# Block-diagonal v in a macaron block: four masked ScalarE copies per chunk become one copy and four SBUF transfers

## The reference

```python
x = x + 0.5 * ffn(layernorm(x))           # 128 -> 512 -> relu -> 128
x = x + attn(layernorm(x))
x = x + 0.5 * ffn(layernorm(x))

q, k, v = split(x @ w_qkv.T)              # 8 heads x 16; blocks c of 32 tokens
qp = elu(q @ proj) + 1;  kp = elu(k @ proj) + 1      # 128 features f
kv   = einsum('bhcsf,bhcsd->bhcfd', kp, v)
num  = einsum('bhcsf,bhcfd->bhcsd', qp, kv)
z    = 1 / (einsum('bhcsf,bhcf->bhcs', qp, kp.sum(3)) + 1e-8)
out  = (num * z) @ w_out.T + b_out
```

## Time and profile before

| | us |
|---|---|
| median of 3 runs (132.30 to 133.36) | 132.82 |
| the profiled execution, its own time | 132.64 |
| its span, first to last instruction | 130.9 |
| PE busy (share) | 120.0 (92%) |
| ScalarE (ACT) busy | 90.3 (69%) |
| VectorE (DVE) busy | 89.6 (68%) |
| GpSimd (POOL) busy | 48.9 (37%) |
| granted TensorE clock | 1.000 |

### The profile page before, as it was taken

The page is one execution under the profiler, slowest core; times in us unless marked ns, Lnnn a source line. Parts: engine busy times, 40 slices in busy tenths (PEclk is TensorE's granted clock), DMA queues, the critical chain, the costliest instruction groups (busy, mean ns, idle before and its releaser), DMA issues.

```text
span 130.9 us, 4453 instructions
## 1 busy us (share of the span) xinstructions
PE 120.0 (92%) x1895; PEld 97.5 (75%) x1895; DVE 89.6 (68%) x223; ACT 90.3 (69%) x154; POOL 48.9 (37%) x54
## 2 busy tenths in 40 slices
PE   5989999959999988999998999999979979999891
PEld 5989989835759845876985685798557768788891
DVE  6899883495697579579569949961993694637411
ACT  4656395788897886878778887888787863351720
POOL 7635669069058049006205910930000048005300
PEclk9999999999999999999999999999999999999999
DMA  3898400993019200002900000570020000200202
GB/s 95 266 250 225 71 3 26 381 178 61 0 56 359 78 0 0 5 5 103 377 6 5 3 5 0 211 270 5 5 80 5 0 8 5 80 0 0 80 6 80
DMA packets 10123, 11.10 MB, mean 85 GB/s; under 512 B 788, under 2 KB 6296, under 8 KB 10104
## 3 DMA queue, kind: packets, MB, share of 16 engines
q1 hardware_dynamic: 9952, 10.75, 26.5%
q10 hardware_dynamic: 152, 0.07, 0.2%
HBM read 2.03 MB, written 1.05 MB: 24 GB/s over the span
## 4 chain that ended last, share of the span: by engine, by line
PE 76%; DVE 10%; ACT 6%; issue 6%; POOL 0%; POOLq 0%; DVEq 0%
PE G L310 17%; PE wide L336 9%; PE SO L347 6%; PE SO L363 5%; ACT expo L642 5%; PE G L319 4%; PE wide L389 4%; PE G L301 3%; PE G L292 3%; PE G L303 3%; PE G L302 3%; PE SO L310 3%; PE G L382 2%; DVE xnT_lo L815 2%; PE wide L301 2%
## 5 line engine op out<-in xcount | busy, mean ns | idle before, releaser
L828 DVE SCALAR_TENSOR_TENSOR feat<-expo,wide 128x1024 f32<-128x1024 f32 x32 | 38.7, 1218 | 19.6 <-ACT expo L642 19.3
L642 ACT ACTIVATE expo<-wide,minus_one 128x1024 f32<-128x1024 f32 x32 | 35.5, 1115 | 8.7 <-PE wide L336 8.6
L987 POOL TENSOR_TENSOR rstd<-var_eps,minus_half 128x4 f32<-128x4 f32 (+1 forms) x15 | 13.5, 899 | 65.5 <-DVE var_eps L801 65.2
L310 PE MATMUL G<-w,hidden 128*128 128x128 f32 x208 | 26.6, 277 | 0.0
L310 PEld LDWEIGHTS G<-w,hidden 128*128 128x128 f32 x208 | 25.1, 192 | 0.7
L336 PE MATMUL wide<-qk_packed,proj_padded 128*128 128x512 f32 x64 | 23.0, 444 | 0.4 <-DVE feat L828 0.3
L623 ACT ACTIVATE hidden<-G,b_cols 128x512 f32<-128x512 f32 (+1 forms) x25 | 16.0, 650 | 4.5 <-PE G L303 3.9
L347 PE MATMUL SO<-feat 128*32 128x32 f32 x1024 | 15.3, 197 | 1.4 <-DVE feat L828 1.3
L347 PEld LDWEIGHTS SO<-feat 128*32 128x32 f32 x1024 | 13.3, 111 | 2.3 <-DVE feat L828 1.7
L363 PEld LDWEIGHTS SO<-v_blocks,scores_sb 128*32 128x32 f32 x256 | 5.2, 108 | 12.3 <-issue 8.4
L363 PE MATMUL SO<-v_blocks,scores_sb 128*32 128x68 f32 x256 | 10.4, 234 | 2.8 <-DVE attn L844 1.8
(11 more groups left out here) (99 smaller groups left out, 193.5 us busy)
## 6 DMA issues: line engine op xcount, KB each, us to landing
qk_packed<-qk_hi SPq DMA_DIRECT2D x16, 256.0 KB, 2.5
qk_packed<-qk_lo SPq DMA_DIRECT2D x8, 256.0 KB, 2.5
qk_packed<-sixteenth SPq DMA_DIRECT2D x2, 512.0 KB, 6.3
x_in<-in_L_attn_x_dram SPq DMA_DIRECT2D x3, 256.0 KB, 5.2
out_dram<-x SPq DMA_DIRECT2D x3, 256.0 KB, 2.2
w<-in_L_ffn_W_dram SPq DMA_DIRECT2D x2, 256.0 KB, 4.1
x_in<-in_L_attn_x_dram SPq DMA_DIRECT2D x2, 128.0 KB, 2.6
proj_padded<-proj_hi SPq DMA_DIRECT2D x4, 64.0 KB, 2.5
```

The lines of the kernel that those rows point to most:

```text
L310: mm = pe.matmul(bank[:, t * D:(t + 1) * D], hidden[f][:, i, t * P:(t + 1) * P], w2[:, i, :], start=(i == 0 and t == tiles[0]), stop=(i == ...
L642: nc.scalar.activation(expo[:, n % 2, :, tokens(c)], wide[n % 2][:, :, tokens(c)], ACT.Exp, bias=minus_one[:, 0:1]).then_inc(exp_done, 1)
L828: nc.vector.scalar_tensor_tensor(out=feat[:, n % FEAT_BUFS, :, tokens(c)], in0=expo[:, n % 2, :, tokens(c)], scalar=1.0, in1=wide[n % 2][: ...
L987: nc.gpsimd.tensor_tensor(rstd[k][:, part], var_eps[k][:, part], minus_half[:, 0:n], ALU.pow).then_inc(rstd_ready[k], 1)
```

## The change

ScalarE copies v once per chunk, unscaled, into the 128-row tensor `v_rows`, whose 17th column holds ones that GpSimd writes once at the start. SP then issues four transfers per chunk (`move_v`), each of which takes the 32 rows of one block j, 4 tiles x 8 heads x 17 columns = 544 elements a row, to the same 32 rows of the operand for block j. The zeros are written once: for buffer 0 by VectorE and GpSimd at the start, for buffer 1 by GpSimd later. `own_block`, its sum and ScalarE's copy of the column of ones go. `v_blocks` now has the block j ahead of tile and head, so that a transfer writes one run per row, and `mix` reads 4 runs of 17 columns where it read 68 in one.

The waits change with it. `mix` of a chunk's first head waits for the four transfers; TensorE waits before the loop for ScalarE's one copy in place of four; ScalarE's copy waits until the transfers of the chunk before have read `v_rows`; SP waits for the zeros, for the copy, and for `mix` of the chunk before the last one (`mixed`). `move_v(c)` stands in SP's order directly behind `move_qk(c)`, so `move_v(0)` is ahead of `move_ones(1)`.

```diff
+        v_rows = sb("v_rows", [P, NT, HEADS, VW])
-        v_blocks = sb("v_blocks", [P, 2, NT, HEADS, NB, VW])
+        v_blocks = sb("v_blocks", [P, 2, NB, NT, HEADS, VW])
...
+            def move_v(c):
+                wait(sp, pool_set, 4)
+                wait(sp, blocks_set[c % 2], 2)
+                wait(sp, v_copied, c + 1)
+                wait(sp, mixed, HEADS * (c - 1))
+                for j in range(NB):
+                    own = slice(j * BLOCK, (j + 1) * BLOCK)
+                    sp.dma_start(v_blocks[own, c % 2, j, :, :, :], v_rows[own, :, :, :]).then_inc(v_moved[c % 2], 16)
...
             move_qk(0)
+            move_v(0)
             move_ones(1)
             for c in range(1, NC):
                 move_qk(c)
+                move_v(c)
...
                 if h == 0:
-                    wait(pe, v_spread, NB * (c + 1))
-                    wait(pe, tails_set, 1)
+                    wait(pe, v_moved[c % 2], 16 * NB * (c // 2 + 1))
...
-                                   v_blocks[:, c % 2, t, h, :, :].rearrange("p j w -> p (j w)"),
+                                   v_blocks[:, c % 2, :, t, h, :],
...
-            pe.wait_ge(v_spread, NB)
+            pe.wait_ge(v_copied, 1)
...
-            def v_spreading(c, bank, part):
+            def v_copy(c, bank):
                 wait(act, v_sum, c + 1)
-                wait(act, mixed, HEADS * (c - 1))
-                for j in part:
-                    nc.scalar.mul(v_blocks[:, c % 2, 0:TILES[c], :, j, 0:HD].rearrange("p t h d -> p (t h) d"),
-                                  bank[:, tokens(c)].rearrange("p (th d) -> p th d", d=HD),
-                                  own_block[:, j:j + 1]).then_inc(v_spread, 1)
+                wait(act, v_moved[(c - 1) % 2], 16 * NB * ((c + 1) // 2))
+                nc.scalar.copy(v_rows[:, :, :, 0:HD].rearrange("p t h d -> p (t h) d"),
+                               bank[:, tokens(c)].rearrange("p (th d) -> p th d", d=HD)).then_inc(v_copied, 1)
...
-                    v_spreading(c + 1, GA, range(0, 2))
-                if s == 5:
-                    v_spreading(c + 1, GA, range(2, NB))
+                    v_copy(c + 1, GA)
...
-            act.wait_ge(masks_set, 1)
-            nc.scalar.copy(v_blocks[:, :, :, :, :, HD].rearrange("p s t h j -> p (s t h) j"),
-                           own_block[:, :].rearrange("p (a j) -> p a j", a=1).broadcast_to([P, 2 * NT * HEADS, NB])
-                           ).then_inc(tails_set, 1)
...
-            v_spreading(0, SO, range(NB))
+            v_copy(0, SO)
...
-            dve.wait_ge(ident_set, 1)
-            nc.vector.tensor_reduce(own_block[:, :], ident.rearrange("p (j q) -> p j q", j=NB),
-                                    mybir.AxisListType.X, ALU.add).then_inc(masks_set, 1)
+            nc.vector.memset(v_blocks[:, 0, 0:NB // 2, :, :, :], 0.0).then_inc(blocks_set[0], 1)
...
             pool.wait_ge(padding_set, 2)
+            nc.gpsimd.memset(v_rows[:, :, :, HD], 1.0).then_inc(pool_set, 1)
+            nc.gpsimd.memset(v_blocks[:, 0, NB // 2:NB, :, :, :], 0.0).then_inc(blocks_set[0], 1)
             reciprocal_root(0, 0)
...
             norm_apply(1, 2, x1[:, :, :])
+            nc.gpsimd.memset(v_blocks[:, 1, :, :, :, :], 0.0).then_inc(blocks_set[1], 2)
             add_bout(1)
```

More of the change, by code:

```diff
@@ L79, in macaron_kernel @@
         proj_padded = sb("proj_padded", [P, 2, HEADS, F], F32R)
-        own_block = sb("own_block", [P, NB])
         b1_rows = sb("b1_rows", [NI, P])
@@ L134, in macaron_kernel @@
         ident_set = sem("ident_set")
-        masks_set = sem("masks_set")
         w1_hi_ready = sem("w1_hi_ready")
@@ L153, in macaron_kernel @@
         v_sum = sem("v_sum")
-        tails_set = sem("tails_set")
-        v_spread = sem("v_spread")
+        blocks_set = [sem(f"blocks_set{i}") for i in range(2)]
+        v_copied = sem("v_copied")
+        v_moved = [sem(f"v_moved{i}") for i in range(2)]
         feat_sum = sem("feat_sum")
@@ L697, in fill_third @@
                 if s == 4:
-                    v_spreading(3, GA, range(0, 2))
-                if s == 5:
-                    v_spreading(3, GA, range(2, NB))
+                    v_copy(3, GA)
                 if s == 5:
```

## The result

The changed kernel takes 133.39 us in the median (20 runs, 133.30 to 134.33) against 132.82 (20 runs, 132.21 to 133.78) before. The ratio is 1.0055, with a 95% interval of 1.0039 to 1.0072: about 0.6 us slower, and within the 1% called no change. The profiled execution took 133.35 us, 0.71 more than the one of before.

What follows compares the result with a forecast made beforehand. TensorE, busy 92% of the span, was taken to bound the kernel. The start-up shift of 1.10 less 0.16 of slack gave 0.94 us; 132.64 + 0.94 = 133.58, rounded to 133.6, all else at 0; range 132.4 to 134.8.

Steps and rivals of the forecast that it cites:

- What goes from ScalarE: ScalarE's 16 scaled copies become 4, freeing about 7.8 us; costed at nothing, as ScalarE follows TensorE.
- VectorE's statistics, +0.79: Start: a memset of 1.00 us replaces a sum that cost 0.21, so VectorE's statistics move by 0.79 us.
- The hold on `var_eps`, +0.31: Start: GpSimd's memset holds up VectorE's first `var_eps` until about 5.39 instead of 5.08, 0.31 us more; other bound 0.
- The second half of the statistics, +1.10: VectorE at the start, after statistics shift and hold: 0.79 + 0.31 = 1.10 us later, also for the second normed tiles.
- GpSimd is no limit of its own: Start: GpSimd's first root ends at 6.24, before the second starts at 6.51, so GpSimd adds no delay.
- The slack ahead of the low part, 0.16: VectorE's low part at 7.53 had 0.16 us of slack waiting for ScalarE, so TensorE at 8.10 moves by 0.94.
- rival (a): Start: the shift is hidden or small, and the time stays at 132.6 to 133.1 us; chance 0.16.
- Nothing absorbed later: From 8.10 to 24.79 us TensorE waits for nobody, and later waits are for engines also moved: shift carried on whole.
- The first mix without a wait: Chunk 0: v lands at 29.7, ahead of the first mix at 30.57; taken as 0, at worst a 2.7 us stall.
- the reads of mix: 256 passes reading 4 runs of 17 columns instead of 68 in a row: taken as 0, bound 2.9 us.
- rival (b): First mix at 30.57: v's transfers come late, ending 1.8 us past 30.84 at half rate, 135.4 us; chance 0.11.
- (c): Reads of mix are slower: 136.5 us at the bound, 134.3 with a quarter of it; chance 0.04.

Runs made afterwards that it cites:

- the twelve copies put back: Changed kernel, but ScalarE makes three more copies of v per chunk into a spare tensor: 133.27 us, ratio 1.0038 to the kernel before.
- the kernel with the zeros behind the roots: Changed kernel, but GpSimd writes the ones and all buffer 0 zeros right behind the first two reciprocal roots: 133.83 us, ratio 1.0078 to the kernel before.
- the gap kernel: Changed kernel, but GpSimd writes the ones and all buffer 0 zeros in its idle time from about 23 us: 132.80 us, again 132.85 us.
- the kernel with VectorE's half of the zeros: Changed kernel, but only VectorE's half stays at the start; GpSimd writes its half and the ones from 23 us: 133.37 us, ratio 1.0050.

## Why the prediction was right

The direction, the place and the mechanism of the forecast hold: VectorE's memset at the start delays the first `ffn_up`, and all behind it. The sizes were too large, and partly they made up for each other, which is luck. Forecast were 0.94 us from the profiled execution, 133.6 us; measured were 0.57 between the medians, 0.71 between the profiles, 133.39 us. At the first `ffn_up` itself it was 0.46.

- What goes from ScalarE, at nothing: right, by its waits for TensorE in the profile and by the twelve copies put back.
- VectorE's statistics, +0.79: measured 4.27 for 3.33, 0.94. The memset's length was right (0.96), the gap of 0.29 us before it was not in the sum, though the row of the memset before it showed 0.27. As the statistics themselves took 0.42 for 0.47, `var_eps` started 0.90 later.
- The hold on `var_eps`, +0.31: the mechanism is shown, but this is the term that was most wrong. The row grew by 0.05, and the second statistics start at 5.09 with or without GpSimd's memset. As VectorE came later than worked out (5.02 for 4.91) and GpSimd's memset ended earlier (5.21 for 5.35), only 0.2 us of it was left. With VectorE's memset gone, the hold was 0.88 us.
- The second half of the statistics, +1.10 by the sum of the two: measured 5.09 for 4.35, 0.74. Besides the hold, the sum missed a slack of 0.16 us in front of them: before, they had begun 0.23 us after the start of `var_eps`, now 0.07. The second half of x explains it. Before, it was issued at 1.21 and landed 3.1 us later, at 4.3, just ahead of these statistics at 4.35; in the profile of the kernel with the zeros behind the roots, the chain names this landing (4.17) as what released them.
- "GpSimd is no limit of its own": right in the changed kernel, where both roots wait for VectorE, but by 0.14 us only (6.14 for 6.00).
- The slack ahead of the low part, 0.16: by the starts it was 0.25. The prediction took the low part to be VectorE's path with a short wait for ScalarE. The chain of before came there from TensorE's passes without use, by way of its transposes, so the argument against rival (a), that nothing on VectorE's path has slack over 0.16 us, did not hold.
- Together: 0.90 less 0.16 is 0.74 at the second statistics, 0.71 at the second normed tiles (6.88 for 6.17), less 0.25 is the 0.46 us that reached TensorE, not 0.94.
- Nothing absorbed later: right up to 52 us to within 0.1.
- The first mix without a wait, and the reads of mix: right. The first mix stood at 31.08, and v landed 2.0 to 2.2 us after its issue where 2.5 were taken. The stall of rival (b), 1.8 us, is absent; with v first, the queue brought all of it in time. By its own terms (279 KB in the 3.94 us from 26.9 to 30.84) it would have decided from 71 GB/s down, not 67; nothing hangs on this.
- Rival (a), start-up hidden: falls. (c), slower reads: falls, 234 ns per pass in both.

## What to carry to other kernels

Work taken from an engine that waits for another one gives nothing; read who waits for whom at each place before counting it. What such a change adds at the very start of a program is paid as far as it exceeds the slack there: here VectorE's statistics moved by 0.94 us and TensorE's first product by 0.46, and that was carried to the end. Follow the chain back from the place, too, not only the last wait in front of it: here it led to another engine's own passes. A buffer's first zeros belong in an idle stretch between the start and their first use. When delays are added up along an engine, subtract the slack ahead of each instruction, by the distance of starts and by the landing of what each one reads, and not only by the idle time shown, and check a memset of GpSimd against every `tensor_scalar` of VectorE that it can run beside.

## What the runs showed of the hardware

A memset on GpSimd, which reads nothing, held VectorE's `tensor_scalar` in SBUF to its own end: 1.05 us for 0.17, and 2.04 for 0.60. Also a `tensor_tensor` with both operands in SBUF and a sum of GpSimd got in each other's way (1.93 for 1.20), and the root queued behind lost 1 us.

Executions start the same way, but TensorE's 22 first passes without use do not end at the same time: at 5.71 us in one profile of the gap kernel, at 6.61 in the other, with the granted clock at 1.00 in both. In the second, the first `ffn_up` was at 8.14, not 7.75, with VectorE's low part waiting 0.54 us for ScalarE. The changed kernel had its first `ffn_up` at 8.56 in two profiles in which these passes ended at 5.64 and 6.62, because VectorE was late in any case. That fits its narrow spread, 17 of 20 executions within 0.13 us, where the kernel before spreads over 1.5. That this is the cause of the spread is an inference. In the profile of the kernel before, they ended at 6.57; had they ended at 5.64, the first `ffn_up` would by an estimate have come at 6.17 + 1.68 = 7.85 in place of 8.10, so they can explain only a part of the 1.5.

In some executions the granted clock falls to 0.50 at about 30.2 us, two us behind an idle time of 1.2 us. Without a further wait it was back at 1.00 before 34 us (the kernel with VectorE's half of the zeros, whose profiled execution took 134.28 us against a median of 133.37); with the wait of 2.55 us for v in that stretch it stayed low until about 40.4. Why it falls in some executions and not in others was not tried.
